# Expert tiles whose gated product is turned by DMA and VectorE instead of TensorE, with the down projection three tiles behind

## The chip, the cores and the metric

One core of a Trainium2 chip runs the kernel. The metric is the time of one execution in device microseconds, as the median of several runs. Lower is better. Everything is float32, made of a high part (fp32r) and a low part where a product needs the accuracy: each such product is three matmuls, high by high, high by low and low by high.

## The reference, cut to what matters

The layer adds causal linear attention and a mixture of experts to its input. The changed part is the mixture:

```
xn = layernorm(x)                                  # 4096 tokens of 256
top_w, top_i = top_k(xn @ Wg, 2); top_w = softmax(top_w)
h = xn @ W1[e];  g = xn @ W2[e]                    # 256 -> 512, 8 experts
y = (silu(h) * g) @ W3[e]                          # 512 -> 256
x + attention(xn) + sum over the 2 chosen experts of top_w * y
```

## The kernel before

**Stages.** The first 300 us or so are the attention, in 32 steps, beside the routing: each token's normalised row is written twice, once for each of its experts, to a scratch in HBM (`xs_d`), sorted by expert within each batch. Then comes the loop over `NT` = 71 tiles of 128 rows, each tile of one expert. Its number stands in the list `texp`, and the tile's row numbers in `glist`. Eight experts change at most seven times over the 71 tiles. In tiles 0 to 7 the engines also split the last weights in high and low parts (`w12_high`, `w12_low`, `w3_high`, `w3_low`).

**One tile, t.** The order on each engine is written out by hand, and semaphores tie the engines together.

- GpSimd (POOL) fetches the 128 rows with an indirect DMA, `gather(t)`, line 485, four tiles ahead of their use, and at the end adds the results to `out` with an accumulating indirect DMA, `scatter(t)`, line 496. A token is in two experts' lists, so two scatters may add to one row. For that reason `scatter(t)` waits until scatter t-1 has landed (`d_sc`).
- TensorE (PE) turns the rows (`transpose_g`, line 1171, 2 transposes), multiplies by W1 and by W2 (`up(t, 0)` and `up(t, 1)`, line 1182, 6 matmuls of 512 columns each), turns the gated product (`transpose_s`, line 1191, 4 transposes into bank 5) and multiplies by W3 (`down`, line 1203, 12 matmuls of 256 columns).
- ScalarE (ACT) rounds the turned rows to `xgh` (line 619), takes the silu of the first product into `hs` (line 638) and rounds the turned product to `sTh` (line 625).
- VectorE (DVE) makes the low parts `xgl` (line 979) and `sTl` (line 988), multiplies the second product into `hs` (line 1009), copies the weights of the rows to `xw` (line 984) and scales the result to `yo` (line 996, two buffers, each free again when its scatter has landed).

**Order around the change.** In turn t the PE runs `up(t, 0)`, `transpose_s(t-1)`, `up(t, 1)`, `transpose_g(t+1)`, `down(t-1)`: the down projection is one tile behind. `hs`, `sTh` and `sTl` have one buffer each. The queue of SyncE (SP) has nothing to do during this loop but to wait for the last scatter. In the attention it moves parts of Q and K within SBUF (lines 313 and 320) and loads x (line 380) and weights.

## Time and profile before

| | |
|---|---|
| median of 3 runs | 669.55 us (668.41 to 669.73) |
| span of the profiled execution, first to last instruction | 665.4 us |
| what the median has beyond that span | 4.15 us |
| PE busy | 641.8 us, 96% of the span |
| DVE, ACT, POOL busy | 410.6, 341.6, 344.1 us |
| chain that ended last | PE 87%, line 1182 alone 29% |
| DMA, 16 engines, software and hardware queues | 22.0% and 20.2% of the span |

The time of the profiled execution is given as its span alone, so the sum of the prediction is made against the span, and the 4.15 us are added at the end. In the tables of the trace, "idle before <- releaser" is how long the engine stood still ahead of an instruction and what ended that. PE is the matmul row, PEld the weight load that overlaps it. Matmuls are pipelined, so their starts tell the pace and their durations overlap.

### The profile page before, as it was taken

Reading aid. Unit: us, or ns where it says so; the run is one execution under the profiler, and the core shown is the slowest. Engines: PE = TensorE matmul, PEld = TensorE weight load, DVE = VectorE, ACT = ScalarE, POOL = GpSimd, SP = SyncE. Lnnn points to the kernel's source line nnn. Section 1 sums busy time; section 2 is a strip of 40 time slices with the busy share of each in tenths; the row PEclk is TensorE's granted clock in tenths of the full one; section 3 lists DMA queues with packets and bytes.
Section 4 is the critical chain, followed back from the end, with each engine's and each line's share of the span. In section 5 each row is a group of like instructions: output and inputs, shape, how many; then the busy total and the mean of one; then the engine's idle time right before and its main releaser. Section 6 shows DMA issues by size and latency. Waiting matters only on the chain.

```text
span 665.4 us, 16423 instructions
## 1 busy us (share of the span) xinstructions
PE 641.8 (96%) x5414; PEld 496.5 (75%) x5414; DVE 410.6 (62%) x1067; ACT 341.6 (51%) x515; POOL 344.1 (52%) x381
## 2 busy tenths in 40 slices
PE   8899999999999999999999999999999999999994
PEld 7555666666666666657888888888888888888883
DVE  6777788787878585777975444444544445444452
ACT  3668878787877686766642232322323223232331
POOL 3265655546463736473465555455545555455542
PEclk9999999999999999999999999999999999999998
DMA  4653555554443435447633434333333433333332
GB/s 134 141 133 99 127 153 130 152 130 147 93 136 77 128 85 154 118 150 249 207 59 58 66 51 66 50 57 60 58 59 50 66 51 57 58 51 58 58 50 25
DMA packets 37775, 64.07 MB, mean 96 GB/s; under 512 B 8289, under 2 KB 25825, under 8 KB 37697
## 3 DMA queue, kind: packets, MB, share of 16 engines
q0 software_dynamic: 16704, 28.12, 22.0%
q1 hardware_dynamic: 20432, 34.24, 20.2%
q8 instruction: 50, 0.82, 0.5%
q10 hardware_dynamic: 560, 0.66, 0.3%
q14 instruction: 29, 0.23, 0.1%
HBM read 27.72 MB, written 22.68 MB: 76 GB/s over the span
## 4 chain that ended last, share of the span: by engine, by line
PE 87%; DVE 4%; DMA 2%; ACT 2%; issue 2%; SPq 1%; ACTq 0%; POOL 0%; POOLq 0%; DVEq 0%
PE banks L1182 29%; PE banks L1203 15%; PE banks L1056 10%; PE banks L1038 8%; PE banks L1076 7%; PE banks L1191 5%; PE banks L1085 4%; PE banks L1120 3%; PE banks L1171 2%; PE banks L1105 1%; PE banks L1111 1%; DMA K<-Kt 1%; ACT T L533 1%; DVE xTl L740 1%; PE banks L1094 1%
## 5 line engine op out<-in xcount | busy, mean ns | idle before, releaser
L496 POOL DMA_INDIRECT out<-yo,xw x71 | 112.2, 1581 | 154.4 <-DVE yo L996 76.6
L625 ACT ACTIVATE sTh<-banks 128x512 fp32r<-128x512 f32 x71 | 42.5, 598 | 192.4 <-PE banks L1191 186.6
L476 POOL TENSOR_SCALAR_AFFINE_SELECT T<-T 128x512 f32<-128x512 f32 x128 | 80.8, 642 | 108.5 <-ACT T L539 43.1
L988 DVE TENSOR_TENSOR sTl<-banks,sTh 128x512 fp32r<-128x512 f32 x71 | 49.0, 691 | 118.9 <-ACT sTh L625 118.9
L1182 PE MATMUL banks<-w12h,xgh 128*128 x284 | 118.0, 415 | 0.6 <-DVE xgl L979 0.6
L1182 PE MATMUL banks<-w12l,xgh 128*128 x284 | 112.2, 395 | 0.0
L1182 PE MATMUL banks<-w12h,xgl 128*128 x284 | 112.1, 395 | 0.0
L485 POOL DMA_INDIRECT xg<-xs_scr,glist x71 | 72.4, 1020 | 21.5 <-issue 20.0
L1056 PE MATMUL banks<-T,vau 128*17 128x512 f32 (+3 forms) x1024 | 75.6, 434 | 0.9 <-POOL T L476 0.9
L467 POOL DMA_INDIRECT xs_scr<-xb,slots x64 | 64.3, 1004 | 18.7 <-issue 10.0
L1038 PE MATMUL banks<-Q,K 32*128 32x256 f32 (+2 forms) x1024 | 70.5, 358 | 3.5 <-DMA K<-Kt 2.2
L525 ACT ACTIVATE T<-banks 128x1024 f32<-128x1024 f32 x64 | 62.1, 1026 | 12.5 <-PE banks L1038 11.9
L533 ACT ACTIVATE T<-banks 128x768 f32<-128x768 f32 x64 | 48.5, 810 | 27.2 <-PE banks L1038 27.2
L1182 PEld LDWEIGHTS banks<-w12h,xgl 128*128 128x128 f32 x284 | 53.3, 188 | 12.0
L1056 PEld LDWEIGHTS banks<-T,vau 128*17 128x17 f32 x1024 | 26.0, 97 | 46.3 <-issue 38.4
L1182 PEld LDWEIGHTS banks<-w12h,xgh 128*128 128x128 f32 x284 | 53.8, 189 | 7.8 <-issue 1.0
L1038 PEld LDWEIGHTS banks<-Q,K 32*128 32x128 f32 x1024 | 38.6, 183 | 27.1 <-ACT T L525 12.7
L1182 PEld LDWEIGHTS banks<-w12l,xgh 128*128 128x128 f32 x284 | 53.9, 190 | 6.3
L996 DVE TENSOR_SCALAR yo<-banks,xw 128x256 f32<-128x256 f32 x71 | 34.3, 483 | 39.0 <-PE banks L1203 31.2
L539 ACT ACTIVATE T<-banks 128x768 f32<-128x768 f32 x64 | 48.7, 810 | 18.0 <-PE banks L1038 16.1
L1009 DVE TENSOR_TENSOR hs<-banks,hs 128x512 f32<-128x512 f32 x71 | 49.1, 692 | 10.2 <-PE banks L1182 0.9
L1203 PE MATMUL banks<-w3h,sTh 128*128 x284 | 51.1, 302 | 0.8 <-ACT sTh L625 0.8
(174 smaller groups left out, 1222.3 us busy)
## 6 DMA issues: line engine op xcount, KB each, us to landing
Q<-Q SPq DMA_DIRECT2D x128, 64.0 KB, 2.4
w12r<-w SPq DMA_DIRECT2D x16, 512.0 KB, 4.2
out<-xa SPq DMA_DIRECT2D x16, 256.0 KB
w3r<-w SPq DMA_DIRECT2D x8, 512.0 KB, 8.7
K<-Kt SPq DMA_DIRECT2D x124, 32.0 KB
xa<-x SPq DMA_DIRECT2D x7, 512.0 KB, 4.7
xg<-xs_scr,glist POOLq DMA_INDIRECT x71
out<-yo,xw POOLq DMA_INDIRECT x71
```

Source lines behind the costliest of these rows:

```text
L467: e.indirect_dma_start(xs_d, bass.IndirectOffsetOnAxis(slots[:, k, 4 * b + blk:4 * b + blk + 1].bitcast(U32), 0), xb[b % 2][:, blk, :], No ...
L476: e.affine_select(out=v, in_=v, pattern=[[0, 4], [1, P]], compare_op=ALU.is_ge, fill=-1.0, base=0, channel_multiplier=-1).then_inc(s["g_mk ...
L485: e.indirect_dma_start(xg[:, t % GR, :], None, xs_d, bass.IndirectOffsetOnAxis(glist[:, t:t + 1].bitcast(U32), 0)).then_inc(s[f"d_g{t % GR ...
L496: e.indirect_dma_start(out, bass.IndirectOffsetOnAxis(xw[:, t % 4, NE:NE + 1].bitcast(U32), 0), yo[:, t % 2, :], None, compute_op=ALU.add) ...
L525: e.activation(T0[n % 2][:, 2 * h:2 * h + 2, :], banks[:, 2 * h:2 * h + 2, :], ACT.Square, scale=0.25, bias=1.0).then_inc(s["a_s"], 1)
L533: e.activation(T1[:, 2 * h:2 * h + 2, :], banks[:, 2 * h:2 * h + 2, 0:384], ACT.Square, scale=0.25, bias=1.0).then_inc(s["a_s"], 1)
L988: e.tensor_tensor(sTl[:], banks[:, 5, :], sTh[:].bitcast(F32), ALU.subtract).then_inc(s["v_st"], 1)
L1009: e.tensor_tensor(hs[:], banks[:, 2 * (t % 2) + 1, :], hs[:], ALU.mult).then_inc(s["v_mu"], 1)
L1038: i = e.matmul(banks[:, r, c0:c0 + w], K2[rr, g, h, jm * P:(jm + 1) * P], Q2[g][rr, h, p, 512 - w:512], start=(p == 0), stop=(p == 1))
L1056: i = e.matmul(banks[32 * r:32 * r + HA, 4, 512 - w:512], vau[b % 2][:, jm, 4 * qd + r, :], v[:, r, :], start=(jm == 0), stop=(jm == 2), s ...
L1182: i = e.matmul(banks[:, 2 * (t % 2) + m, :], a[:, k, :], w[:, bass.ds(expert[t] * 4 + (2 * k + m), 1), :], start=(k == 0 and n == 0), stop ...
L1203: i = e.matmul(banks[:, 6 + t % 2, 0:256], a[:, k * P:(k + 1) * P], w[:, bass.ds(expert[t] * 4 + k, 1), :], start=(k == 0 and n == 0), sto ...
```

## The change

For tiles 8 to 68 (`TS` = 8, `TE` = 69, 61 tiles) the PE no longer turns the gated product. SP moves it within SBUF with four DMAs per tile (`move_h`), each from all 128 partitions, 128 values of each, to 32 partitions of `hq`. That puts every 32x32 block where a transpose within blocks finishes the job, and VectorE does this with one instruction from `hq` into bank 5 (`turn_s`). The order of tokens and hidden units that comes out is put right by the access patterns `s_bank`, `s_turned`, `h_bank`, `h_turned`, and by another order of W3's rows on the host. `hs`, `hq`, `sTh` and `sTl` have two buffers. The down projection is three tiles behind (`LAG`), and after the last tile three of them stand in a row. Tiles 0 to 7 and 69, 70 are turned on the PE as before.

Scatters use two semaphores, and two may be in flight. Two tiles of one expert share no token, so only where the expert changes must scatter t wait for t-1; VectorE writes a list of the counts to wait for (`holds`), and POOL loads one of them for each tile (`hold`). Padding rows go to two spare blocks in turn. Gathers run further ahead in POOL's order. The program is built with `dynamic_dma_scratch_size=4096`, an argument that was not given before.

```diff
+            def move_h(t):
+                e.wait_ge(s["v_mu"], t + 1)
+                if t >= TS + 2:
+                    e.wait_ge(s["v_th"], t - TS - 1)
+                for r in range(4):
+                    e.dma_start(hq[32 * r:32 * r + 32, t % 2, :],
+                                hs[:, t % 2, P * r:P * r + P]).then_inc(s[f"d_hq{t % 2}"], 16)
...
+            def hold(t):
+
+                if t == 3:
+                    e.wait_ge(s["v_hold"], 1)
+                else:
+                    e.wait_ge(s["g_hold"], t - 3)
+                count = 16 * ((t - 1) // 2)
+                landed = e.value_load(held[0:1, t - 1:t], min_val=count, max_val=count + 16)
+                e.wait_ge(s[f"d_sc{(t - 1) % 2}"], landed)
+                e.tensor_tensor(mark[:], minus[:], minus[:], ALU.add).then_inc(s["g_hold"], 1)
+
             def scatter(t):
+                if t >= 3:
+                    hold(t)
                 e.wait_ge(s["v_yo"], t + 1)
...
-                    e.wait_ge(s["d_sc"], 16 * t)
...
+                    e.wait_ge(s[f"d_sc{t % 2}"], 16 * (t // 2))
...
             for t in range(NT):
-                if t + GR < NT:
-                    gather(t + GR)
+                upto = t + 4 if t == 0 else t + 5 if t < TS else t + 7
+                while ahead <= min(upto, NT - 1):
+                    gather(ahead)
+                    ahead += 1
                 scatter(t)
...
+            def turn_s(t):
+                e.wait_ge(s[f"d_hq{t % 2}"], 64 * ((t - TS) // 2 + 1))
+                e.wait_ge(s["v_st"], t)
+                e.transpose(banks[:, 5, :], hq[:, t % 2, :]).then_inc(s["v_th"], 1)
...
+            def holds():
+
+                e.wait_ge(s["c_hold"], 2)
+                then(e.tensor_tensor(change[:, 0:71], tf[:, 1:72], tf[:, 0:71], ALU.subtract))
+                then(e.scalar_tensor_tensor(held[:, 0:71], change[:, 0:71], 16.0, before[:, 0:71], ALU.mult, ALU.add), "v_hold")
```

In `scalar_program` silu(t) now waits, from tile 10 on, for the move of tile t-2 out of the same half of `hs` (`d_hq`), and in turn t the order is silu(t), `xgh`(t+1), `sTh`(t-2). SP loads W3's last two units after `v_hold` instead of after `v_te`. Some small constants are added at the start.

**TensorE, an ordinary tile in the middle of the loop, where up(t, 0) ends and up(t, 1) begins.** Before:

```order
L1182 MATMUL banks<-w12h,xgl 128x512
L1191 MATMUL banks<-ident,hs 128x128 x4
L1182 ISA
L1182 MATMUL banks<-w12h,xgh 128x512
L1182 REGISTER_ALU
L1182 MATMUL banks<-w12l,xgh 128x512
```

After the change, the same place, and then the place between tiles 9 and 10 (line 1279 is `transpose_g`, 1316 the load of the tile's expert, 1290 `up`, 1311 `down`):

```order
L1290 MATMUL banks<-w12h,xgl 128x512
L1290 ISA
L1290 MATMUL banks<-w12h,xgh 128x512
L1290 REGISTER_ALU
L1290 MATMUL banks<-w12l,xgh 128x512
```

```order
L1290 MATMUL banks<-w12h,xgl 128x512
L1279 MATMUL banks<-ident,xg 128x128 x2
L1316 TENSOR_LOAD texp
L1316 ISA x2
L1290 ISA
L1290 MATMUL banks<-w12h,xgh 128x512
```

The four transposes are gone between the two halves of `up`; behind `transpose_g` of tiles 10 and 11 no down projection stands, since `down(8)` comes only in turn 11.

**VectorE, one turn in the middle of the loop.** Before:

```order
L988 TENSOR_TENSOR sTl<-banks,sTh 128x512
L1009 TENSOR_TENSOR hs<-banks,hs 128x512
L979 TENSOR_TENSOR xgl<-banks,xgh 128x256
L984 COPY xw<-xg 128x16
L991 TENSOR_LOAD texp
L991 ISA x2
L996 ISA
L996 TENSOR_SCALAR yo<-banks,xw 128x256
```

After:

```order
L1105 TENSOR_TENSOR hs<-banks,hs 128x512
L1071 TENSOR_TENSOR xgl<-banks,xgh 128x256
L1076 COPY xw<-xg 128x16
L1081 STREAM_TRANSPOSE banks<-hq 128x512
L1088 TENSOR_LOAD texp
L1088 ISA x2
L1093 ISA
L1093 TENSOR_SCALAR yo<-banks,xw 128x256
L1085 TENSOR_TENSOR sTl<-banks,sTh 128x512
```

The transpose stands behind `xw` and ahead of `yo`, and `sTl` has moved from ahead of `hs` to the end of the turn; in turn t it is `hs`(t), `xgl`(t+1), turn(t-2), `yo`(t-3), `sTl`(t-2).

**GpSimd, one turn in the middle of the loop.** Before:

```order
L485 DMA xg<-xs_scr,glist 128x272
L496 DMA out<-yo,xw 4224x256
L485 DMA xg<-xs_scr,glist 128x272
L496 DMA out<-yo,xw 4224x256
L485 DMA xg<-xs_scr,glist 128x272
```

After:

```order
L565 DMA out<-yo,xw 4352x256
L539 DMA xg<-xs_scr,glist 128x272
L549 TENSOR_LOAD held
L549 ISA x2
L551 TENSOR_TENSOR mark<-minus 128x4
L565 DMA out<-yo,xw 4352x256
```

Between gather and scatter stand now a load of the count, the wait for it and a small addition.

## Rows read from the trace of the kernel before

**Rows 1.** The page: span, busy time by engine
```profile
span 665.4 us, 16423 instructions
PE 641.8 (96%) x5414; PEld 496.5 (75%) x5414; DVE 410.6 (62%) x1067; ACT 341.6 (51%) x515; POOL 344.1 (52%) x381
```
**Rows 2.** Windows, 411 to 640 us: length, busy by engine, PEclk, DMA share, GB/s
```profile
411.00:640.00 229.00, 229.00 (x1409) 199.66 (x1408) 107.51 (x235) 69.25 (x141) 120.90 (x94) 1.00 0.36 57
```
**Rows 3.** Timeline of ScalarE: start, length; sTh of two tiles, fifteen tiles apart
```profile
353.15 0.60 ACT L625 ACTIVATE sTh<-banks 128x512 fp32r<-128x512 f32 x1 [2.88 <-PE banks L1191]
...
426.29 0.60 ACT L625 ACTIVATE sTh<-banks 128x512 fp32r<-128x512 f32 x1 [2.87 <-PE banks L1191]
```
**Rows 4.** Timeline of all engines over one tile
```profile
562.28 0.40 PE L1182 MATMUL banks<-w12h,xgl 128*128 x1
...
562.32 1.58 POOL L496 DMA_INDIRECT out<-yo,xw  x1 [2.12 <-DVE yo L996]
562.51 0.60 PE L1191 MATMUL banks<-ident,hs 128*128 128x128 f32 x4
...
563.19 0.39 PE L1182 MATMUL banks<-w12l,xgh 128*128 x1
...
563.65 0.59 ACT L638 ACTIVATE hs<-banks 128x512 f32<-128x512 f32 x1
...
564.21 0.99 POOL L485 DMA_INDIRECT xg<-xs_scr,glist  x1 [0.30 <-issue]
564.35 0.38 PE L1171 MATMUL banks<-ident,xg 128*128 128x128 f32 x2
...
564.49 0.72 PE L1203 MATMUL banks<-w3h,sTh 128*128 x4
564.62 0.69 DVE L1009 TENSOR_TENSOR hs<-banks,hs 128x512 f32<-128x512 f32 x1
...
565.23 0.41 DVE L979 TENSOR_TENSOR xgl<-banks,xgh 128x256 fp32r<-128x256 f32 x1
...
565.56 0.16 DVE L984 COPY xw<-xg 128x16 f32<-128x16 f32 x1
...
566.01 0.40 PE L1182 MATMUL banks<-w12h,xgh 128*128 x1
...
566.32 0.48 DVE L996 TENSOR_SCALAR yo<-banks,xw 128x256 f32<-128x256 f32 x1 [0.60 <-PE banks L1203]
```
**Rows 5.** Line 313, SP moves within SBUF: length of an issue, time to landing
```profile
L313 SPq DMA_DIRECT2D Q<-Q x128: 507/589/1620, 14.3 to 276.5; - x128
...
DMA to landing us min/median/max: 2.2/2.4/3.4
```
**Rows 6.** Line 380, SP loads x in 1 KB packets: length of an issue
```profile
L380 SPq DMA_DIRECT2D xa<-x x4: 379/380/380, 91.1 to 196.6; - x4
```
**Rows 7.** DMA queues, 196.5 to 201.5 us, hardware queue: packets, MB, share of 16 engines
```profile
q1 hardware_dynamic: 528, 0.52, 36.6%
```
**Rows 8.** DMA queues, 450 to 655 us, software queue: packets, MB, share of 16 engines
```profile
q0 software_dynamic: 7942, 10.98, 34.3%
```
**Rows 9.** Timeline of GpSimd, two scatters in a row, each held by the last
```profile
406.79 1.58 POOL L496 DMA_INDIRECT out<-yo,xw  x1 [1.77 <-DMA out<-yo,xw]
...
411.34 1.58 POOL L496 DMA_INDIRECT out<-yo,xw  x1 [1.67 <-DMA out<-yo,xw]
```
**Rows 10.** Timeline of all engines around tile 1
```profile
315.80 0.74 PE L1203 MATMUL banks<-w3h,sTl 128*128 x4 [0.40 <-DVE sTl L988]
...
316.26 0.41 DVE L979 TENSOR_TENSOR xgl<-banks,xgh 128x256 fp32r<-128x256 f32 x1
...
316.89 0.49 PE L1182 MATMUL banks<-w12h,xgh 128*128 x1 [0.35 <-DVE xgl L979]
```
**Rows 11.** Timeline of all engines at the end
```profile
652.20 0.63 PE L1203 MATMUL banks<-w3h,sTh 128*128 x4
...
659.25 1.55 POOL L496 DMA_INDIRECT out<-yo,xw  x1 [3.00 <-DMA out<-yo,xw]
```

More of the change, by code:

```diff
@@ L17 @@
 GR = 4
+TS = 8
+TE = NT - 2
+LAG = 3
+XR = 8
 XW = D + NE + 8
@@ L144, in build @@
         pidx = keep.take("pidx", 2, I32)
-        pf = keep.take("pf", 2)
+        pf = keep.take("pf", 3)
         warm = keep.take("warm", 1)
@@ L157, in build @@
         banks = ctx.enter_context(nc.psum_tensor("banks", [P, 8, 512], F32))
-        rm = Region(344, A0)
+        rm = Region(344, Q1)
         xg = rm.take("xg", GR * XW, F32, (GR, XW))
-        xgh = rm.take("xgh", 256, F32R, (2, P))
-        xgl = rm.take("xgl", 256, F32R, (2, P))
-        hs = rm.take("hs", 512)
-        sTh = rm.take("sTh", 512, F32R)
-        sTl = rm.take("sTl", 512, F32R)
-        yo = rm.take("yo", 512, F32, (2, D))
-        xw = rm.take("xw", 64, F32, (4, 16))
-        rq = Region(344, A0)
+        sTh = rm.take("sTh", 1024, F32R, (2, 512))
+        sTl = rm.take("sTl", 1024, F32R, (2, 512))
+        yo = rm.take("yo", 512, F32, (2, D))
+        rx = Region(Q1, A0)
+        hs = rx.take("hs", 1024, F32, (2, HID))
+        at_hq = rx.at
+        hq = rx.take("hq", 1024, F32, (2, HID))
+        xgh = rx.take("xgh", 256, F32R, (2, P))
+        xgl = rx.take("xgl", 256, F32R, (2, P))
+        xw = rx.take("xw", XR * 16, F32, (XR, 16))
+        held = rx.take("held", 72, I32)
+        mark = rx.take("mark", 4)
+        rh = Region(at_hq, at_hq + 1024)
+        before_i = rh.take("before_i", 72, I32)
+        before = rh.take("before", 72)
+        change = rh.take("change", 72)
+        rq = Region(344, Q1)
         K2 = rq.take("K2", 2048, F32R, (2, 2, 512))
@@ L245, in build @@
         sm = r8.take("sm", 32, F32, (2, 4, 4))
+        far = r8.take("far", 8)
         q9 = w12_lo(9)
@@ L402, in sync_program @@
             load_w12(15)
-            e.wait_ge(s["d_sc"], 16 * NT)
+            def move_h(t):
[5 more added lines that the diff above has]
+                                hs[:, t % 2, P * r:P * r + P]).then_inc(s[f"d_hq{t % 2}"], 16)
+            for t in range(TS, TE):
+                move_h(t)
+            for u in range(2):
+                e.wait_ge(s[f"d_sc{u}"], 16 * ((NT + 1 - u) // 2))
         def gpsimd_program(e):
@@ L505, in gpsimd_program @@
             e.wait_ge(s["d_xs1"], 512)
-            e.wait_ge(s["d_z"], 32)
-            for t in range(GR):
-                gather(t)
+            e.wait_ge(s["d_z"], 80)
+            ahead = 0
             for t in range(NT):
-                if t + GR < NT:
-                    gather(t + GR)
+                upto = t + 4 if t == 0 else t + 5 if t < TS else t + 7
+                while ahead <= min(upto, NT - 1):
+                    gather(ahead)
+                    ahead += 1
                 scatter(t)
@@ L621, in high_s @@
             def high_s(t):
-                e.wait_ge(s["p_st"], t + 1)
-                if t:
-                    e.wait_ge(s["p_yo"], t)
-                e.activation(sTh[:], banks[:, 5, :], ACT.Copy).then_inc(s["a_st"], 1)
+                if t < TS:
+                    e.wait_ge(s["p_st"], t + 1)
+                elif t < TE:
+                    e.wait_ge(s["v_th"], t - TS + 1)
+                else:
+                    e.wait_ge(s["p_st"], TS + t - TE + 1)
+                if t >= 2:
+                    e.wait_ge(s["p_yo"], t - 1)
+                e.activation(s_turned(sTh, t), s_bank(t), ACT.Copy).then_inc(s["a_st"], 1)
             e.activation(warm[:, 0:1], pf[:, 0:1], ACT.Silu)
@@ L1014, in vector_program @@
                     w3_low(0)
+                    holds()
                 if t + 1 < NE:
@@ L1222, in tensor_program @@
             step("o", LAST, 1)
-            for t in range(1, NT + 1):
-                if t < NT:
-                    expert_of(t)
-                    up(t, 0)
+            for t in range(1, NT):
+                expert_of(t)
+                up(t, 0)
                 if t == 1:
@@ L1229, in tensor_program @@
                         e.wait_ge(s[f"m{m}"], USED[m])
-                transpose_s(t - 1)
-                if t < NT:
-                    up(t, 1)
+                if t <= TS or t == TE + 1:
+                    transpose_s(t - 1)
+                up(t, 1)
                 if t + 1 < NT:
                     transpose_g(t + 1)
-                if t <= NE:
-                    e.wait_ge(s["v_tl"], t)
-                down(t - 1)
+                if t <= TS:
+                    if t <= NE:
+                        e.wait_ge(s["v_tl"], t)
+                    down(t - 1)
+                elif t - LAG >= TS:
+                    down(t - LAG)
+            transpose_s(NT - 1)
+            for t in range(NT - LAG, NT):
+                down(t)
         with nc.Block() as block:
```

114 lines of the change are left out of this document (80 added, 34 removed).

## The prediction

> **What bounds the kernel now.** I read the page first, then the windows over the tile loop, then the timeline of one tile, and only then the queues. The page says that PE is busy for 641.8 of 665.4 us [rows 1]. That is a mean over stages, so the loop has to be looked at alone: from 411 to 640 us PE is busy for all 229.00 us at a granted clock of 1.00, DVE for 107.5, ACT for 69, POOL for 121, the DMA engines for 0.36 [rows 2]. The waits of ACT, DVE and POOL there are waits for the PE. Fifteen tiles take 426.29 - 353.15 = 73.14 us, 4.876 us per tile [rows 3]. Of this time only what leaves the PE's queue counts.
>
> **The transposes that go.** Within `up` matmuls start 0.23 us apart. The last one of up(t, 0) starts at 562.28, so the next could start at 562.51; there the four transposes start. The second matmul of up(t, 1) starts at 563.19, its first would so have stood at 562.96 without the small gap that the change of weights leaves [rows 4]. From 562.51 to 562.96 are 0.45 us per tile. For 61 tiles that is 27.45 us, and a tile would take 4.43 us. This is the whole gain. The other terms are what it costs.
>
> **DVE, hidden.** Per tile DVE now has 0.69 (`hs`) + 0.69 (`sTl`, as many elements) + 0.41 + 0.16 + 0.48 = 2.43 us [rows 4], and gets a 128x512 transpose from SBUF to PSUM. No row shows one. The nearest is `hs`, as many elements, 0.69 us. As bounds I take 0.48 (`yo`, half the elements) and twice 0.69, 1.38; I take 0.69. The sum is 3.1, at most 3.8 of 4.43 us. Order matters more than the sum. Behind up(t, 1) `hs` and `xgl` come as before, and `xgl`, which lets the next `up` start, ends at 565.64, while that `up` starts at 566.01 [rows 4]: the transpose is put behind it and doesn't touch this margin. Then follow in time the transpose to about 566.4, `yo` to 566.9, ACT's `sTh` (no longer than 0.6 us unless the strided reading of the bank costs) to 567.1 and `sTl` to 567.9. The next `hs` is due at 564.62 + 4.43 = 569.05. There is 1.1 us of room, enough for the 1.38 of a slow transpose (plus 0.7) or for a slow `sTl`, not for everything at once.
>
> **The moves, hidden if they land in time.** SP's queue is empty here. Four issues of 0.59 us [rows 5] are 2.4 us of 4.43; an issue that moved eight times as much took 0.38 [rows 6]. SP waits for `hs`(t) and for turn(t-2), behind nothing but the next tile's moves. The engines: in the window with a load of x, 36.6% of 5 us on 16 engines over 528 packets is 55 ns per 1 KB packet [rows 7]. A tile's moves are 512 packets of 512 bytes and 64 signals; at 28 to 55 ns that is 1.0 to 2.0 us of each engine. The gathers and scatters take 34.3% of 4.876, 1.67 us [rows 8]. Together 2.7 to 3.7 of 4.43 us: full, not over. The latency L from the first issue to the last landing decides. From below: three issues at 0.38 and 2.2 to land, 3.3 us. From above: three at 0.59, the longest landing of 3.4, and behind a tile's worth of other traffic, 1.67: 6.8. With the medians it is 3 x 0.59 + 2.4 = 4.2 [rows 5, 6, 8]; I take 4.5, near the medians, since the moves in those rows also ran beside other transfers. What L may be follows from a loop over two tiles: move(t-2) lands, silu(t) 0.59, `hs` 0.69, `xgl` 0.41, `xw` 0.16, transpose 0.69, then SP may issue move(t) into the same buffer. With four hand-overs of about 0.1 us that is 3.0 + L for two tiles. It holds 4.43 us as long as L is under 5.9.
>
> A row first: moves of 64 KB issued 0.6 us apart each land after 2.4 us [rows 5], so their latencies overlap. The Trainium skill, page "DMA: Bandwidth & Descriptors", section "Measured", calls transfers under 64 KB descriptor-dominated, its rules want one large transfer, and its anatomy section fits 2.0 us fixed plus the bytes, an estimate of 2.15 us for 64 KB. That agrees with the 2.4; paid one after another, as the rule fears, four would make L 8.6 us and a tile 5.8, paid overlapped they leave the sum as it is.
>
> **POOL, probably hidden.** A turn is now scatter 1.58, gather 0.99, and 0.30 of hand-over behind each [rows 4]: 3.17 us. `hold` adds h. The rows have no load of a register on POOL alone; from below I take 0.30, one more hand-over, from above 1.58, another scatter's length; I take 0.8, between, as one load, one wait and one tiny addition are less work than building 128 descriptors. It stays hidden up to 4.43 - 3.17 = 1.26 us. The Trainium skill ("DMA: Bandwidth & Descriptors", "Latency and other measured facts") puts a register load at about 600 ns at least; with that h would be near 0.9 and the sum the same, and no row here shows it.
>
> **Scatters.** Serial ones start 411.34 - 406.79 = 4.55 us apart when each waits for the last [rows 9]. That hides under 4.88 but not under 4.43, so without two in flight 61 x 0.12 = 7.3 us of the gain would go. At the changes of expert, at most seven, one such wait of 4.55 us remains, 0.1 late, and the two `yo` buffers take it up: nothing. The gathers stay more than one tile ahead of need, nothing. The constants at the start fall where DVE and POOL stand waiting for x, nothing.
>
> **The seam at tile 8.** Turns 9 and 10 have no down projection. From the end of up(t, 1), 564.35, to the end of `xgl`, 565.64, plus 0.22 us from there to the next `up` (316.67 to 316.89), are 1.51 us, in which the PE has only the 0.14 of `transpose_g` [rows 4, 10]. It idles 1.37 us twice: +2.7 us. This work isn't saved; it is moved to the end.
>
> **holds().** At tiles 0 and 1 DVE is late: the PE waits 0.40 for `sTl` and 0.35 for `xgl` [rows 10]. Two small instructions more, each 0.16 [rows 4] up to 0.41 with its wait, go straight to the path: 0.3 to 0.8, I take +0.5. The same delays the loads of W3's last units by 1 us, which are needed many tiles later: nothing.
>
> **The end.** From the end of the last `up`, 652.20, to the end of the span are 13.2 us; the last scatter starts at 659.25 and the rest takes 6.15 [rows 11]. After the change two more down projections stand behind that point (2 x 1.44 us less ahead of it: -2.9). I follow the scatters: `yo`(67) can be ready 2.2 us behind the last `up`, its scatter starts at 2.6; scatter(68) at 5.1; `yo`(69) needs buffer 67 to have landed, 4.5 us behind its start: scatter(69) at 8.0; likewise scatter(70) at 10.5, and the end at 16.7. That is +3.5, net +0.6; between -0.5, if scatters overlap better, and +2.5.
>
> **Sum.** 665.4 - 27.45 + 2.7 + 0.5 + 0.6 = 641.8 us of span; with the 4.15 us around it **645.9 us**, a gain of 3.5%.
>
> **The rivals.**
> 1. *Part of the gain is eaten each tile.* One of the loops is a little over 4.43: L between 5.9 and 6.75, h between 1.26 and 1.7, or scatters that in practice follow one another. The last has a row, 4.55 us [rows 9]: 645.9 + 7.3 = 653. With L = 6.4 a tile takes (6.4 + 3.0) / 2 = 4.7 and the time is 645.9 + 61 x 0.27 = 662. For it speak the DMA engines at up to 80%, and a POOL that has never done such a load; against it the 1.4 us between L of 4.5 and its limit.
> 2. *The moves become the bound, slower than before.* The loop of silu, `hs`, transpose and move sets the pace from L = 6.75 us on, where it makes 4.876. My upper bound of 6.8 just reaches it. If scatter packets stretch the moves to 7.5 us, a tile takes 5.25, and the time is 645.9 + 61 x 0.82 = 696. The place is silu(t) on ACT, waiting for the DMA of two tiles ago, and behind it in ACT's queue `xgh`, on which the next `up` waits. Against it: the longest of 128 landings is 3.4.
> 3. *The page's rule holds*, the four moves pay one after another: L = 8.6, 5.8 us per tile and 729 us. The rows speak against it; it is in rival 2's chance.
> 4. *The PE doesn't get shorter*: something else of 0.45 us (the load of weights behind the last `up`, no longer covered by a transpose's) takes the place. 669 to 673 us. Every matmul of `up` has its own weights loaded ahead of it, and 0.23 us apart is their pace inside `up`, so I see no reason for one between its halves.
>
> **How the numbers follow.** Forecast, 642 to 650 us: 0.70. Rival 1, 650 to 668: 0.18, two thirds of it under 658. Rivals 2 and 3: 0.06. Rival 4, or a loop that lands on 4.88: 0.02. Under 642, if the seam and the end cost nothing (665.4 - 27.45 + 4.15 = 642.1 is the floor): 0.04. The range 642 to 658 leaves out 0.04 + 0.06 + 0.06 + 0.02 = 0.18. A difference of 0.2%, 1.3 us, is about what a measurement can tell from none. Faster 0.90, same 0.03, slower 0.07.
>
> **What would show it.** In the profile after: `sTh` starts every 4.43 us and PE without idle in the windows; two idle stretches of 1.4 us ahead of `up` at tiles 10 and 11; the transpose near 0.69 us; silu never released by the DMA into `hq`, and the last of four landings 4 to 5 us behind the first issue; POOL with `yo` as the releaser of its scatters. I am wrong if silu or the transpose wait for the DMA (rival 2 or 1), if POOL's scatter is released by "issue" and `yo` waits for the DMA into `out` (h too long), or if the PE's transposes of bank 5 turn out to have cost less than 0.45.

## The result, and the profile after

The changed kernel took 643.9 us (median of four runs, 643.4 to 645.7) against 669.1 us (668.4 to 669.7) before on the same chip: a ratio of 0.962, 95% interval 0.960 to 0.964. That is 3.8% faster, where 645.9 us and 3.5% were forecast. In a later set of runs on another chip it took 642.8 us, ratio 0.962 (0.960 to 0.965).

The page of the kernel after, the lines that answer to [rows 1], with the clock that TensorE was granted in 40 slices of the span:

```profile
span 644.0 us, 16648 instructions
...
PE 617.4 (96%) x5170; PEld 475.2 (74%) x5170; DVE 450.4 (70%) x1134; ACT 348.4 (54%) x515; POOL 358.4 (56%) x453
...
PEclk8799999999999999999999999999999999999998
```

PE has 244 matmuls fewer (61 times 4) and is as full as before. DVE has gained 40 us and POOL 14 us; the windows and timelines below show that PE doesn't wait for either in the loop. (The page's chain that ended last gives PE 44%, "issue" 25% and POOL 17% after, where it gave PE 87% before. That walk goes backwards along POOL's queue; yet POOL stands idle some 1.2 us ahead of an ordinary scatter, waiting for `yo`, so it doesn't set the pace.) What is new is the second digit of PEclk. Windows over the start show it (length, busy time of PE, PEld, DVE, ACT and POOL, PEclk, DMA share, GB/s). First the kernel after:

```profile
0.00:40.00 40.00, 33.50 (x264) 25.11 (x265) 26.53 (x86) 19.59 (x26) 11.44 (x43) 0.87 0.49 128
```

Then the kernel before, the same stretch:

```profile
0.00:40.00 40.00, 34.03 (x302) 25.23 (x306) 29.48 (x96) 21.78 (x29) 13.62 (x43) 1.00 0.50 126
```

In this execution of the changed kernel PE issued 264 instead of 302 instructions in the first 40 us, at a mean granted clock of 0.87, so part of the time at the lower of its two levels, 1.2 instead of 2.4 GHz. In a second profiled execution of the same kernel (e10 below) the clock there was 1.00. It is a difference between executions, not one between kernels, and it has to be taken out before the loop is compared. I cut the span at the first and at the last silu (ACT, into `hs`). Source view of the silu, before:

```profile
L638 ACT ACTIVATE hs<-banks x71: 590/594/598, 307.6 to 651.5; 128x512 f32<-128x512 f32 x71
```

After:

```profile
L716 ACT ACTIVATE hs<-banks x71: 587/598/601, 312.6 to 627.1; 128x512 f32<-128x512 f32 x71
...
  DMA hq<-hs: 21.2, 24
...
  DVE hs L1105: 2.6, 2
```

(minimum, median, maximum in ns, start of the first and of the last. The second row puts 21.2 us of ACT's idle time, in 24 pieces, down to the DMA into `hq`; part of it is a wait for the PE, as shown below. The third says that DVE in turn waited for the silu, 2.6 us in all, twice.)

| us, one execution each | before | after | after again (e10) | after as forecast |
|---|---|---|---|---|
| up to the first silu | 307.6 | 312.6 | 306.2 | 307.6 |
| first to last silu | 343.9 | 314.5 | 315.7 | 316.8 |
| last silu to the end | 13.9 | 16.9 | 16.8 | 17.4 |
| span | 665.4 | 644.0 | 638.7 | 641.8 |
| time of that execution | not given | 645.7 | 640.45 | |

The forecast of the loop is 343.9 - 27.45 + 2.7 + 0.5 - 2.9 (two down projections that now come behind the last silu); of the end it is 13.9 + 3.5. The loop lost 28 to 29 us, the end got 3 us longer, and the start moves by 6 us from one execution to the next. Of the 1.2 us between the two loops after, 1.0 lies in tiles 0 to 2 (12.5 and 13.5 us from the first silu to the third); from the third silu to the last it is 302.0 and 302.2 us after and 332.0 before.

**The pace.** Timeline of ScalarE after, `sTh` of two tiles that lie 44 tiles apart (start, length, what ended the idle time before):

```profile
405.59 0.60 ACT L700 ACTIVATE sTh<-banks 128x512 fp32r<-128x512 f32 x1 [1.24 <-DVE banks L1081]
...
599.44 0.60 ACT L700 ACTIVATE sTh<-banks 128x512 fp32r<-128x512 f32 x1 [1.24 <-DVE banks L1081]
```

193.85 / 44 = 4.406 us per tile, against 4.876 in [rows 3] and a forecast of 4.43. The releaser is no longer the PE's transposes but DVE's. In the windows view the PE is never idle:

```profile
500.00:520.00 20.00, 20.00 (x123) 17.63 (x122) 13.30 (x28) 6.70 (x13) 12.57 (x14) 1.00 0.67 124
```

DVE's busy share went from 0.47 [rows 2] to 0.67, the DMA engines' from 0.36 to 0.67 in these 20 us and 0.62 from 411 to 600 us.

**One tile and what surrounds it.** Timeline of all engines after, the rows that answer to [rows 4]:

```profile
500.74 0.99 POOL L539 DMA_INDIRECT xg<-xs_scr,glist  x1 [0.30 <-issue]
500.75 0.69 DVE L1105 TENSOR_TENSOR hs<-banks,hs 128x512 f32<-128x512 f32 x1 [1.31 <-PE banks L1290]
...
501.75 0.21 POOL L551 TENSOR_TENSOR mark<-minus 128x4 f32<-128x4 f32 x1
501.76 0.72 DVE L1081 STREAM_TRANSPOSE banks<-hq 128x512 f32<-128x512 f32 x1
...
502.50 0.48 DVE L1093 TENSOR_SCALAR yo<-banks,xw 128x256 f32<-128x256 f32 x1
502.52 0.60 ACT L700 ACTIVATE sTh<-banks 128x512 fp32r<-128x512 f32 x1 [1.24 <-DVE banks L1081]
...
503.26 1.59 POOL L565 DMA_INDIRECT out<-yo,xw  x1 [1.30 <-DVE yo L1093]
503.30 0.39 PE L1290 MATMUL banks<-w12h,xgl 128*128 x1
...
503.52 0.39 PE L1290 MATMUL banks<-w12h,xgh 128*128 x1
503.72 0.60 ACT L716 ACTIVATE hs<-banks 128x512 f32<-128x512 f32 x1 [0.61 <-PE banks L1290]
503.75 0.39 PE L1290 MATMUL banks<-w12l,xgh 128*128 x1
...
507.71 0.39 PE L1290 MATMUL banks<-w12h,xgl 128*128 x1
...
508.13 0.60 ACT L716 ACTIVATE hs<-banks 128x512 f32<-128x512 f32 x1 [0.61 <-DMA hq<-hs]
...
509.57 0.69 DVE L1105 TENSOR_TENSOR hs<-banks,hs 128x512 f32<-128x512 f32 x1 [1.32 <-PE banks L1290]
```

- The last matmul of up(t, 0) starts at 503.30, the first of up(t, 1) at 503.52: 0.22 us apart, no gap where the transposes stood. The second of up(t, 1) starts at 503.75, 0.45 us behind the last of up(t, 0), where [rows 4] has 563.19 - 562.28 = 0.91. Over the tiles in the middle of the loop the medians of this step are 0.902 us before and 0.453 after. The rest of the tile takes 3.97 us before and 3.95 after, and that 0.02 lies in the next four steps of up(t, 1) (0.924 and 0.907 us).
- `hs` of a tile is written from 500.75. The transpose of two tiles ago ends at 502.48, and SP may then move this tile's `hs` out. The silu at 508.13 is the one that overwrites the same half of `hs`, so the move has landed by then, and L, from the first issue to the last landing, is at most 5.5 us here, where I had taken 4.5. The row names the DMA as releaser, but the last matmul of up(t, 0) ends at 507.71 + 0.39 = 508.10, and the silu starts 0.03 us behind it, just as the silu at 503.72 does, for which the row names the PE. It would have started at 508.13 without any move. Read like this, 47 of the 61 silus that follow a move start at most 0.04 us behind the PE, and only 14 are late, by 0.14 to 0.98 us, 8.5 us in all; their L is 5.6 to 6.5 us. From below: in the median tile the last mark on record of the move's semaphore comes 4.9 us behind the first issue (some marks are missing, so it may be later). So L is 4.9 to 5.5 us in most tiles.
- That silu ends at 508.73, and the `hs` behind it starts only at 509.57, when the PE is done. It could be 0.8 us later before DVE lost time.
- POOL's tiny addition (`mark`), which follows the load of the register and the wait, starts at 501.75, while the gather, 0.99 long, started at 500.74: load and wait don't show, and `hold` costs POOL about 0.2 us. The load itself takes 0.3 us (source view below); the one behind the scatter of 503.26 starts at 503.55, while that scatter is still running.

Source views after of the move, of the transpose and of the register load in `hold`:

```profile
L445 SPq DMA_DIRECT2D hq<-hs x244: 547/602/2002, 356.3 to 623.4; - x122
```

```profile
L1081 DVE STREAM_TRANSPOSE banks<-hq x61: 712/722/909, 365.3 to 629.6; 128x512 f32<-128x512 f32 x61
```

```profile
L549 POOLq TENSOR_LOAD <-held x68: 284/306/545, 337.6 to 637.2; - x68
```

An issue takes 0.60 us, so four take 2.4 [rows 5: 0.59]; the last lands 3.0 to 3.6 us behind its own issue (4.9 to 5.5, less 1.9), against 2.4 in [rows 5]. The transpose is 0.72 us (0.69 forecast).

DMA queues after, 450 to 600 us (packets, MB, share of 16 engines), which answer to [rows 8] and, for the moves, to [rows 7]:

```profile
q0 software_dynamic: 6531, 9.20, 39.7%
q1 hardware_dynamic: 19584, 8.92, 21.8%
```

The moves take 0.218 x 150 x 16 / 19584 = 26.7 ns of an engine for each packet: my lower bound, 28. The gathers' and scatters' packets take 146 ns where they took 142 before (0.343 x 205 x 16 / 7942). Together 0.615 x 4.406 = 2.7 us per tile.

**The seam and the end.** Timeline of PE and what precedes it after, between tiles 9 and 10:

```profile
359.72 0.38 PE L1279 MATMUL banks<-ident,xg 128*128 128x128 f32 x2
...
361.16 0.49 PE L1290 MATMUL banks<-w12h,xgh 128*128 x1 [1.06 <-DVE xgl L1071]
```

361.16 - 359.72 - 0.14 = 1.30 us are lost, and the next tile has the same: 2.6 us (2.7 forecast). The end, timeline of the PE and of POOL after, which answers to [rows 11]:

```profile
628.69 0.65 PE L1311 MATMUL banks<-w3h,sTh 128*128 x4
...
631.33 1.55 POOL L565 DMA_INDIRECT out<-yo,xw  x1 [2.93 <-DVE yo L1093]
...
633.67 1.55 POOL L565 DMA_INDIRECT out<-yo,xw  x1 [0.56 <-DVE yo L1093]
...
637.42 1.55 POOL L565 DMA_INDIRECT out<-yo,xw  x1 [1.97 <-DVE yo L1093]
...
639.37 1.55 POOL L565 DMA_INDIRECT out<-yo,xw  x1 [0.16 <-issue]
```

The last four scatters start 2.3, 3.8 and 2.0 us apart, two always in flight, and the span ends 15.3 us behind the last `up`, at 628.69 (16.7 forecast, 13.2 before).

### The profile page after: what moved, and what is told of

It is laid out like the page before. It is cut to its first block, busy times and chain, and to the rows that moved or that the text cites. A ratio compares the mean times of both kernels' runs of the same rounds, so it can differ in the third digit from the quotient of the medians.

```text
span 644.0 us, 16648 instructions
## 1 busy us (share of the span) xinstructions
PE 617.4 (96%) x5170; PEld 475.2 (74%) x5170; DVE 450.4 (70%) x1134; ACT 348.4 (54%) x515; POOL 358.4 (56%) x453
## 4 chain that ended last, share of the span: by engine, by line
PE 44%; issue 25%; POOL 17%; DVE 4%; DMA 3%; ACT 3%; POOLq 2%; SPq 1%; ACTq 0%; DVEq 0%
PE banks L1164 10%; PE banks L1146 8%; POOL xg L539 8%; PE banks L1184 8%; POOL out L565 6%; PE banks L1290 4%; PE banks L1193 4%; PE banks L1228 3%; POOL mark L551 2%; POOLq L549 2%; PE banks L1311 2%; PE banks L1213 1%; ACT T L603 1%; PE banks L1219 1%; DMA K<-Kt 1%
## 5 line engine op out<-in xcount | busy, mean ns | idle before, releaser
L1290 PE MATMUL banks<-w12h,xgh 128*128 x284 | 112.7, 397 | 2.9 <-DVE xgl L1071 2.8
L521 POOL DMA_INDIRECT xs_scr<-xb,slots x64 | 64.1, 1002 | 20.2 <-issue 12.6
L716 ACT ACTIVATE hs<-banks 128x512 f32<-128x512 f32 x71 | 42.4, 597 | 48.5 <-DMA hq<-hs 21.2
L1290 PEld LDWEIGHTS banks<-w12h,xgl 128*128 128x128 f32 x284 | 53.3, 188 | 11.7
L689 ACT ACTIVATE xgh<-banks 128x256 fp32r<-128x256 f32 x71 | 27.2, 383 | 59.6 <-PE banks L1279 43.2
L1085 DVE TENSOR_TENSOR sTl<-banks,sTh 128x512 fp32r<-128x512 f32 x71 | 48.9, 690 | 13.2 <-ACT sTh L700 10.9
```

Of the source, the lines that this page charges most:

```text
L521: e.indirect_dma_start(xs_d, bass.IndirectOffsetOnAxis(slots[:, k, 4 * b + blk:4 * b + blk + 1].bitcast(U32), 0), xb[b % 2][:, blk, :], No ...
L1290: i = e.matmul(banks[:, 2 * (t % 2) + m, :], a[:, k, :], w[:, bass.ds(expert[t] * 4 + (2 * k + m), 1), :], start=(k == 0 and n == 0), stop ...
```

## The experiments

**Theory A**, the prediction's: the gain is the PE's transposes, 0.45 to 0.47 us for each tile that is turned elsewhere; the moves, DVE's transpose and the loads of the register lie beside the PE; two scatters in flight earn nothing by themselves, but the shorter tile needs them. **Rival B**: a good part of the gain comes from the reordering (lag of three tiles, gathers further ahead, two scatters in flight), and the transposes are worth less than they look. About the margin of the moves there were two more readings: of the two-tile loop through L, whose limit the trace puts near 6.3 us, and of the DMA engines, at 0.62 to 0.67.

### e1, e2: how many tiles are turned by moves

```diff
-TS = 8
+TS = 40    # e1: 29 tiles moved instead of 61; e2 has TS = 66: 3 tiles
```

> The first tile that is moved and turned by VectorE is 40 instead of 8, so 29 tiles instead of 61 leave out the four transposes of TensorE. Theory A (the gain is those transposes, 0.47 us a tile on TensorE's queue, since the changed kernel runs a tile in 4.406 us against 4.876): 643.9 + 32 x 0.47 = 658.9 us, and within one profile tiles up to 39 run at 4.88 and the later ones at 4.41 us. Rival B (the gain comes from the later down projection and from two scatters in flight): about 644 to 647 us, and the early tiles are already faster than 4.88.

Measured: 659.55 us (657.7 to 660.2), ratio 0.985 (0.983 to 0.988).

> Only tiles 66, 67 and 68 are moved and turned by VectorE; two scatters in flight, the run-ahead of the gathers, the double buffers and the seam with two turns without a down projection stay. Theory A: 643.9 + 58 x 0.47 = 671.2 us, a little slower than before, since the seam (2.6 us) and holds() (0.4 us) stay without a gain. Rival B: clearly under 669, some 655 us.

Measured: 671.2 us (668.4 to 674.4), ratio 1.0035 (1.001 to 1.006).

Within the one kernel e1 both paces stand side by side. Timeline of ScalarE, `sTh` before and behind tile 40:

```profile
505.30 0.60 ACT L700 ACTIVATE sTh<-banks 128x512 fp32r<-128x512 f32 x1 [2.88 <-PE banks L1299]
510.17 0.60 ACT L700 ACTIVATE sTh<-banks 128x512 fp32r<-128x512 f32 x1 [2.87 <-PE banks L1299]
...
526.41 0.60 ACT L700 ACTIVATE sTh<-banks 128x512 fp32r<-128x512 f32 x1 [1.23 <-DVE banks L1081]
530.81 0.60 ACT L700 ACTIVATE sTh<-banks 128x512 fp32r<-128x512 f32 x1 [1.23 <-DVE banks L1081]
```

4.87 us with the transposes on the PE, 4.40 without. Two scatters in flight and `hold` are there in both. The lag of three tiles and the further gathers aren't: in the code they begin at `TS` (`if t <= TS: ... down(t - 1)`, `t + 5 if t < TS else t + 7`), so the tiles ahead of 40 in e1 and ahead of 66 in e2 have the old order on the PE, and the gathers run less far ahead than in the changed kernel, also in e2, whose expectation says that their run-ahead stays. What these two could earn has to be read from the trace. The step from the last matmul of up(t, 0) to the second of up(t, 1), where the transposes stand, takes 0.902 us ahead of tile 40 and 0.453 behind it (medians); the four steps behind it take 0.925 and 0.907; the remaining 3.05 us of the tile, `down` among them, differ by 0.002. The PE doesn't stand still in either stretch, so there was no wait that another order could have taken away. From 3 to 29 moved tiles the ratio falls by 0.0183, 12.2 us or 0.47 us per tile, and from there to the 61 of the changed kernel (0.9623) by 0.0229, 15.3 us or 0.48 per tile. Rival B is out: the two scatters in flight earn nothing by themselves (e2 is 0.35% slower than before), and the lag and the gathers leave no trace in a tile outside the transposes' place. A has the pace, and this slope.

### e3: scatters one after another again

```diff
-                if t >= 3:
-                    hold(t)
                 e.wait_ge(s["v_yo"], t + 1)
...
-                    e.wait_ge(s[f"d_sc{t % 2}"], 16 * (t // 2))
+                    e.wait_ge(s[f"d_sc{(t - 1) % 2}"], 16 * ((t - 1) // 2 + 1))
```

> The changed kernel, but every scatter waits until the one before has landed, and hold with its load and its small addition on GpSimd is gone. By the row of before (4.55 us from one serial scatter to the next) a tile takes 4.55 instead of 4.41 us and VectorE's yo waits for the DMA: 643.9 + 61 x 0.145 + about 1 at the end = 653 to 655 us. If the moves in flight make a scatter land later, more: 4.7 us a tile is 662. Rival: two in flight are not needed, or hold costs what they bring: 644 us.

Measured: 671.4 us (667.3 to 676.5), ratio 1.0047 (1.002 to 1.008). The whole gain is gone, where I had expected 7 us of it to go. Timeline of GpSimd in e3, two scatters in a row in the loop, and the last four:

```profile
508.22 1.58 POOL L561 DMA_INDIRECT out<-yo,xw  x1 [1.82 <-DVE yo L1089]
...
512.92 1.59 POOL L561 DMA_INDIRECT out<-yo,xw  x1 [1.83 <-DVE yo L1089]
```

```profile
648.99 1.55 POOL L561 DMA_INDIRECT out<-yo,xw  x1 [4.14 <-DVE yo L1089]
653.46 1.55 POOL L561 DMA_INDIRECT out<-yo,xw  x1 [2.92 <-DVE yo L1089]
657.79 1.55 POOL L561 DMA_INDIRECT out<-yo,xw  x1 [2.78 <-DVE yo L1089]
662.47 1.55 POOL L561 DMA_INDIRECT out<-yo,xw  x1 [3.12 <-DMA out<-yo,xw]
```

And what `yo` waits for in e3 (source view; the kernel after has 3.0 us, 2 times, in this place):

```profile
  DMA out<-yo,xw: 95.5, 48
```

The same cut as above, with the kernel after beside it: up to the first silu 311.3 (after: 312.6), first to last silu 326.2 (314.5), last silu to the end 29.5 (16.9). So 11.7 us of the 23.0 between the two spans go in the loop and 12.6 at the end (1.3 come back at the start).

In the loop a scatter starts 4.70 us behind the last one, not the 4.55 of [rows 9]: 0.29 above the tile's 4.41, and not 0.12. The moves aren't to blame. Timeline of GpSimd before, three scatters on, each held by the last:

```profile
436.61 1.58 POOL L496 DMA_INDIRECT out<-yo,xw  x1 [1.81 <-DMA out<-yo,xw]
...
450.53 1.58 POOL L496 DMA_INDIRECT out<-yo,xw  x1 [1.74 <-DMA out<-yo,xw]
```

That is 13.92 / 3 = 4.64 us each without any move. Over all scatters that start as soon as the last has landed, the kernel before has a median of 4.64 and a mean of 4.73 us (41 of them, two at 6.0), e3 4.65 and 4.69 us (59). The pair in [rows 9] was among the short ones. The first 21 moved tiles or so don't feel it (`sTh` at 364.66 and 457.18 us: 4.41 each), since buffers let the scatters fall behind for a while; the 39 behind them take 4.71 (to 640.79), and 39 x 0.30 = 11.7. At the end the scatters are late and can't catch up. The fourth from last starts 648.99 - 637.5 = 11.5 us behind the last silu (after: 631.33 - 627.1 = 4.2), `down` of the last tile waits 2.84 us until `yo` frees its bank, and from that scatter on it takes 18.0 us to the end (12.7), 4.3 to 4.7 us per scatter where the kernel after has 2.0 to 3.8. The ratios differ by 4.2%, 28 us, some 5 more than these two executions. Most of that is which executions were profiled: 645.7 us is 1.8 above the median of the changed kernel, 668.8 is 2.6 below that of e3, whose runs spread over 9 us.

### e4, e5: more moves per tile

One, and three, more moves of 16 KB each (128 partitions, 32 values) from the same half of `hs` into a spare buffer, ahead of the four; silu and transpose wait for them too.

```diff
+                for r in range(1):    # e5: range(3)
+                    e.dma_start(spare[:, t % 2, r, :], hs[:, t % 2, P * r:P * r + 32]).then_inc(s[f"d_hq{t % 2}"], 16)
...
-                    e.wait_ge(s[f"d_hq{t % 2}"], 64 * ((t - 2 - TS) // 2 + 1))
+                    e.wait_ge(s[f"d_hq{t % 2}"], 80 * ((t - 2 - TS) // 2 + 1))    # e5: 112, and in turn_s alike
```

> Ahead of the four moves of each tile SyncE issues a fifth small one of 16 KB to an unused place, on which silu and the transpose also wait; the landing comes one issue, about 0.6 us, later. In the changed kernel the moves take 5.5 us from the first issue to the release of silu, and silu could start about 1 us later without harm. Theory: no change, 643 to 646 us, a tile 4.41 us, while silu's waits for the DMA, 21 us in all, grow to 40 or more. Rival (the moves already set the pace, and the 4.41 us is half of a loop of moves): 0.3 us a tile more, 662 us.

Measured: 648.6 us (647.2 to 648.8), ratio 0.970 (0.968 to 0.972): 4.7 us above the changed kernel, where at most 2 were expected.

> Three small moves ahead of the four of each tile instead of one, so the four land about 1.7 us later than in the changed kernel. One extra move gave 648.6 us: most tiles stayed at 4.41 us, some lost 0.2 to 1 us. Theory (the loop of silu, hs, transpose and move takes 2.5 us beside the latency L, which is 5.5 us in the changed kernel): L = 7.2, (7.2 + 2.5) / 2 = 4.85 us a tile, 643.9 + 61 x 0.44 = 671 us, as slow as before the change. Rival (only the order on SyncE's queue counts, seven issues of 0.6 us are 4.2 of 4.41 us): 650 us.

Measured: 666.4 us (663.4 to 671.1), ratio 0.997 (0.995 to 1.000): 23 us above the changed kernel, where 27 were expected.

Source view of the silu in e5, what ended the idle time before it, and who waited for it:

```profile
  DMA hq<-hs: 108.0, 60
...
  DVE hs L1108: 93.3, 51
```

In 60 of the 61 tiles whose silu follows a move the silu stood waiting for the move (here it starts more than 0.1 us behind the PE's last matmul in all 60), and in 51 DVE for the silu. That is the loop of rival 2. Its size can be read too: in the changed kernel, from the start of the silu to the issue of the move are 0.60 us, a hand-over, 500.75 to 502.48 for `hs`, `xgl`, `xw` and the transpose, and a hand-over: 2.5 us. At 4.41 per tile L may be 8.81 - 2.5 = 6.3. The three extra issues of e5 take 1.9 us (0.60 each in the median, and gaps), which by the expectation's working makes L about 7.4 and a tile 4.95. Measured were 4.82 in the mean (`sTh` at 365.27 and, 48 tiles on, at 596.64 us), most between 4.4 and 5.0, some 5.5 to 6.2. The loop is right, its two sizes are not: from the first issue to the silu are 6.7 us, since the last move lands 2.5 us behind its own issue here, and from the silu to the next issue into the same buffer 2.9, together (6.7 + 2.9) / 2 = 4.8. In e4 the one extra issue takes 0.5, which makes L at most 6.0; the 50 silus that are late there start 6.1 us behind the first issue in the median, 3.6 behind the last one. That is still under 6.3, and in e4 most tiles do take 4.41. Some don't. Timeline of SP's queue in e4, three tiles' moves, and what followed the middle one:

```profile
385.95 2.57 SPq L448 DMA_DIRECT2D hq<-hs  x4
...
390.52 3.48 SPq L448 DMA_DIRECT2D hq<-hs  x4
...
394.75 2.54 SPq L448 DMA_DIRECT2D hq<-hs  x4
```

```profile
396.96 0.60 ACT L719 ACTIVATE hs<-banks 128x512 f32<-128x512 f32 x1 [2.19 <-DMA hq<-hs]
...
398.77 0.49 PE L1293 MATMUL banks<-w12h,xgh 128*128 x1 [0.41 <-DVE xgl L1074]
```

Now and then four issues take 0.9 us longer (one single issue of the changed kernel took 2.0 us, the maximum of its source view). With L = 6.0 there is no room for that and the PE idles; with at most 5.5 there is 0.8 us. What makes an issue late is open.

### e6: the extra move, and the transpose earlier

Is it the loop, or are it the queue and the DMA engines, which have one move more? e6 keeps e4's extra move and shortens the loop: DVE does the transpose of tile t-2 ahead of `hs`(t) instead of behind `xw`, so that it no longer stands between `hs`(t) and its move.

```diff
+                if TS <= t - 2 < TE:
+                    turn_s(t - 2)
                 ... hs(t) ...
                 ... xgl(t+1), xw(t+1) ...
-                if TS <= t - 2 < TE:
-                    turn_s(t - 2)
```

> The one extra move stays, and VectorE's transpose of tile t-2 stands ahead of hs(t) instead of behind xgl(t+1) and xw(t+1), where VectorE waits for TensorE anyway. SyncE may then issue the moves of tile t right behind hs(t), about 1 us earlier. Theory (the 4.7 us that the extra move cost are silu waiting for the moves): back to 643 to 645 us, and silu's waits for the DMA, 68 us in all with the extra move, fall below 20. Rival (the extra move costs through the DMA engines or SyncE's queue itself): 648 to 649 us as with the extra move alone.

Measured: 640.8 us (639.4 to 641.8), ratio 0.959 (0.955 to 0.962). Source view of the silu in e6:

```profile
  DMA hq<-hs: 12.3, 6
```

6 waits instead of 49 in e4, and in the loop `sTh` comes every 4.40 to 4.41 us, but for one pair (4.52 and 4.29). From the third silu to the last are 302.0 us as in the changed kernel, where e4 has 306.8. The 4.7 us of e4 were the loop's. The DMA engines carry the extra move at no cost that shows. By its ratio e6, with one move more, is no slower than the changed kernel (0.962).

### e7, e8, e9, e10: what the seam and the end are worth

e7 turns tiles 6 and 7 by moves too, and gives `yo` a third buffer, so that in the end a `yo` waits for the scatter of three tiles ago. e8 does this from tile 4. e9 is e7 with the transpose ahead of `hs`. e10 is the changed kernel once more, beside e9.

```diff
-TS = 8
+TS = 6     # e8: 4
...
+        yo2 = rx.take("yo2", 256)
+        def yo_of(t):
+            return (yo[:, 0, :], yo[:, 1, :], yo2[:])[t % 3]
...
-                if t >= 2:
-                    e.wait_ge(s[f"d_sc{t % 2}"], 16 * (t // 2))
+                if t >= 3:
+                    e.wait_ge(s[f"d_sc{(t - 3) % 2}"], 16 * ((t - 3) // 2 + 1))
...
+                    if t - LAG < NE:
+                        e.wait_ge(s["v_tl"], t - LAG + 1)
```

> The changed kernel with the first moved tile 6 instead of 8 and a third buffer for yo. Two tiles less with transposes on TensorE are 2 x 0.47 = 0.9 us; at the end yo(69) and yo(70) need not wait for a scatter to land, which takes one yo and its hand-over, 0.8 us, off the chain of scatters: 643.9 - 1.7 = 642.2 us. Rival: VectorE, which still splits weights in tiles 6 and 7, delays the two turns without a down projection, and the gain is 0.8 us or less.

Measured: 640.1 us (638.8 to 641.5), ratio 0.958 (0.955 to 0.961).

> As the run before with the first moved tile 4. By the price of a tile 0.9 us less again, 641.3 us. But in tiles 4 to 6 VectorE splits two parts of weights per tile (2 x 1.22 us) beside its 3.15 us: 5.6 us against 4.41 us. Expected: nothing gained over the first tile 6, 642 to 644 us, with TensorE idle ahead of up in turns 5 to 7.

Measured: 640.2 us (638.8 to 644.6), ratio 0.958 (0.954 to 0.962).

> First moved tile 6, three buffers for yo, and VectorE's transpose of tile t-2 ahead of hs(t), without the extra move. A tile stays at 4.405 us, which is TensorE's own work, so the earlier transpose gains only at the seam and the end, about 0.8 us by the profile of the run that had it, beside the 1.7 us of the other two edits: 643.9 - 2.5 = 641.4 us by the time of the changed kernel, 638 to 640 us by the last runs, and 2 to 4 us under the changed kernel beside it. Rival: the edits share what they gain at the end, and it is no faster than with the first moved tile 6 and three yo buffers alone (ratio 0.958).

Measured: 640.3 us (637.5 to 642.5), ratio 0.957 (0.954 to 0.960).

> The changed kernel once more, unaltered, beside the run before on the same chip: 643 to 644 us, ratio 0.962 to the kernel before.

Measured: 642.8 us (640.5 to 643.3), ratio 0.962 (0.960 to 0.965).

e7 to e9 lie 0.4 to 0.5% under the changed kernel, 2.5 to 3 us, but the intervals touch, and none of them is faster for certain. The cut of their profiled executions supports 1.5 to 2 us of it. From the first to the last silu they take 314.7, 315.3 and 314.5 us (changed kernel: 314.5 and 315.7), which looks like no gain. But the first execution of the changed kernel was 1 us quicker in tiles 0 to 2 than e7 to e10 all were (12.5 against 13.4 to 13.5 us), which no edit explains. From the third silu to the last the changed kernel has 302.0 and 302.2 us, e7 301.3, e8 301.8 and e9 301.1: e7 and e9 are 0.7 to 1.2 us shorter, about the 2 x 0.47 us expected of two tiles. From the last silu to the end are 15.9, 16.0 and 16.4 us (16.9 and 16.8): 0.4 to 1.0 us, where the third `yo` buffer was to help. The PE still idles twice for 1.06 us at the seam, only earlier.

e8 wasn't slower than e7, as had been expected: the PE idles at its seam only twice, for 1.12 us each, so VectorE's two parts of weights per tile cost almost nothing there. Its two further tiles don't show either, but one `sTh` in its loop comes 5.69 us behind the last, 1.3 us late, which would hide most of them.

## Why the prediction was right, point by point

1. **What bounds.** Right: PE, and what leaves its queue leaves the time. e1 shows it inside one program, 4.87 and 4.40.
2. **The transposes.** Right: 0.47 us per tile for 0.45, or 28.7 us for 27.45. At their own place 0.902 us became 0.453, which is the 0.45. The other 0.02 are the next four steps of up(t, 1), 4 to 5 ns shorter each; why is open.
3. **DVE.** Right: 0.72 us for 0.69, and hidden where it was put.
4. **The moves.** The mechanism was right, two sizes were off and in part made up for each other, which was luck. L is 4.9 to 5.5 in most tiles and not 4.5: the term that was too small is the landing, 2.4 from [rows 5], which the last of four moves takes 3.0 to 3.6 us for here. The rest of the loop is 2.5 and not 3.0, since DVE's instructions start before the one ahead has ended (four of them, 1.99 us of durations, take 1.73 from 500.75 to 502.48). So the limit is 6.3 and not 5.9, and the margin was some 0.8 us instead of 1.4. What I said would show me wrong, a silu that waits for the DMA, stands in the profile 24 times with 21 us; in truth 14 silus were late, by 8.5 us, and it cost the path next to nothing (DVE waited for the silu twice, 2.6 us in all). The sign alone wasn't a test, for two reasons: a silu named as waiting for the DMA may have been due for the PE at the same moment, and it has slack behind it too. e4 and e5 show where the slack ends. Four overlapping moves did agree with the row: paid one after another they would have given 8.6 us. The Trainium skill, page "DMA: Bandwidth & Descriptors", section "Measured", calls transfers under 64 KB descriptor-dominated, for loads from HBM issued by GpSimd. It doesn't say that the latencies of several transfers add up; that was my reading of it, in rival 3, and L of at most 5.5 us shows that they don't here.
5. **DMA engines.** 2.7 us of each tile's time, the lower end of 2.7 to 3.7.
6. **POOL.** Better than forecast: h is 0.2 us and not 0.8, since the load and the wait for the count run while the scatter before is still going on, and the tiny addition starts 0.02 us after the gather's end. The Trainium skill, page "DMA: Bandwidth & Descriptors", section "Latency and other measured facts", gives a register load a floor of about 600 ns; here the load's own row has 306 ns in the median of 68, 284 at least. The trace of before had such a load too, on VectorE (line 991, 304 ns in the median), from which the prediction could have taken it.
7. **Seam, holds, end.** 2.6 for 2.7. For `holds` the PE waits 0.92 us for `sTl` at tile 1 (0.93 in e10), where it waited 0.40 [rows 10]: 0.52 for 0.5. One small term was missing: the `sTh` of tiles 4 and 5 are 5.2 us apart in every execution of the changed kernel and of e1 to e3, and 4.88 before, 0.3 us whose cause is open. The end is 15.3 us behind the last `up` for 16.7: the scatters overlap better, as the low bound had it, so with two down projections less ahead of it the end is -0.8 net and not +0.6.
8. **The time around the span.** Wrong in name, right in use. 4.15 us was the median of before less the span of one execution. In every profiled run since, the time is only 1.7 to 2.1 us over the span. The other 2.4 us say that the execution on the page of before, all at clock 1.00, was faster than the median one, and such an offset the changed kernel has too (e10's profiled execution took 640.45 us, its median is 642.8): with the start of before its profiled execution would be 644.0 - 5.0 + 1.7 = 640.7 us, and the median is 643.9. So the error of 2.0 us in the sum is 2.8 us that points 2 and 7 were too careful by (641.8 of span, 639.0 measured with that start), less 0.8 of offset.
9. **The rivals.** Rival 1's scatters: right that two in flight are needed, wrong by a factor of three in price, 23 us between the two spans instead of 7.3. Two terms failed: the spacing, 4.55 from a single pair, where serial scatters are 4.7 apart in the mean before and in e3 alike, and the end, where the prediction took only the loop's loss, and serial scatters that have fallen behind can't catch up. The expectation of e3 had the 4.7, but for another reason, moves that delay a scatter; that isn't what the rows show. Rival 2 didn't occur, and e5 shows its loop at work: at L = 6.7 the gain is all but gone. Rival 3 fell with an L of at most 5.5, rival 4 with e1. So both parts had to come together: e2 (two scatters in flight, hardly a tile moved) and e3 (all tiles moved, scatters serial) are each worth nothing alone.

## What to carry to other kernels

When work leaves the bounding engine, list everything that was hidden under the old length of a turn, and compare each with the new one: here a chain of 4.7 us under 4.88 cost nothing, and against 4.41, with what piled up at the end, all of the gain. Take the length of such a chain from many pairs, not from one: the one pair read here was 4.55. A wait in the trace isn't a loss until someone waits for the waiter, and where two things are due at the same moment the name in the row may be the wrong one: compare the start with the end of each. Measure the margin by adding to the suspected step until the time moves (here one issue of 0.5 us moved it a little, three of 0.6 fully). And subtract two executions stage by stage, not span by span: the start alone differed by 6 us between two executions of one kernel.

## What the runs showed of the hardware

- VectorE transposes 128x512 fp32 within 32x32 blocks, from SBUF into a bank of PSUM, in 722 ns; a two-operand product of that size takes 692.
- Four moves of 64 KB within SBUF, issued 0.60 us apart beside gathers and scatters, have all landed 4.9 to 5.5 us behind the first issue in most tiles, although their packets of 512 bytes take an engine 26.7 ns each and the engines are busy for 0.62 of the time. e4 and e6 differ in the order on VectorE, not in what the engines carry, and only e4 loses time. Why the last one takes 3.0 to 3.6 us, where moves in the attention took 2.4 and the last of e5's seven 2.5, isn't explained. In e9, where the same four are issued about 1 us earlier in the tile, their last packet ends 3.5 us behind the first issue in the median tile and 4.5 in the changed kernel, so what runs beside them seems to matter.
- Serial accumulating scatters of 128 rows of 1 KB are 4.64 us apart in the median without moves beside them and 4.65 with them. With two in flight the last ones are 2.0 to 3.8 apart.
- POOL's register load takes 306 ns in the median and runs while the indirect DMA ahead of it is still going on.
- The granted clock in the first 40 us was between 0.87 and 1.00, and differed between executions of the same kernel too. Where it was 0.87 the first silu came at 312.6, 312.3 (e2) and 309.8 us (e9), where it was 1.00 mostly at 306 to 308 us, but in e1 at 311.6: the clock of these 40 us isn't all of it, and the rest stays open.
